# Another order of nodes over the partitions in a three-pass graph kernel: blocks of 32 nodes become runs of 8

## The reference

```python
h = relu(ln(x))
x = x + (adj.T @ h) / adj.sum(axis=0)[:, None]     # layer 0
h = relu(ln(x))
x1 = silu((adj @ h) @ W + b)                       # layer 1, first multiplication
x2 = silu((adj @ x1) @ W + b)                      # layer 1, second multiplication
return x + x2
```

## Time and profile before

| | |
|---|---|
| median of three runs | 654.42 us (653.28 to 654.83) |
| profiled execution, its own time | 653.19 us |
| its span, first to last instruction | 651.3 us |
| mean granted TensorE clock | 0.992 of full speed |
| PE, PEld, DVE, ACT, POOL busy | 627.0, 402.9, 504.0, 298.5, 562.0 us |
| moved by DMA | 199.82 MB |

### The profile page before, as it was taken

The page is one execution under the profiler, slowest core; times in us unless marked ns, Lnnn a source line. Parts: engine busy times, 40 slices in busy tenths (PEclk is TensorE's granted clock), DMA queues, the critical chain, the costliest instruction groups (busy, mean ns, idle before and its releaser), DMA issues.

```text
span 651.3 us, 6791 instructions
## 1 busy us (share of the span) xinstructions
PE 627.0 (96%) x2232; PEld 402.9 (62%) x2232; DVE 504.0 (77%) x518; ACT 298.5 (46%) x372; POOL 562.0 (86%) x283
## 2 busy tenths in 40 slices
PE   7889999999997989999999999999999999999996
PEld 5356666567574456566667667666666666665664
DVE  3988889888847889687777877777787968966982
ACT  1475433543442164645445445445444435433452
POOL 2389899499786579998999999999999999996994
PEclk8999999999998999999999999999999999999999
DMA  8999999999999999999999999909999999999971
GB/s 269 355 374 333 338 336 361 312 328 358 325 280 342 288 343 348 331 315 286 347 347 311 348 347 323 281 2 217 313 346 333 324 318 343 343 320 292 327 234 33
DMA packets 155827, 199.82 MB, mean 307 GB/s; under 512 B 5520, under 2 KB 138896, under 8 KB 155792
## 3 DMA queue, kind: packets, MB, share of 16 engines
q1 hardware_dynamic: 91568, 136.07, 66.4%
q10 hardware_dynamic: 64224, 63.32, 33.0%
HBM read 197.26 MB, written 2.10 MB: 306 GB/s over the span
## 4 chain that ended last, share of the span: by engine, by line
PE 65%; POOL 16%; issue 8%; DMA 6%; DVE 3%; ACT 1%; SPq 1%; POOLq 0%; DVEq 0%; ACTq 0%
PE dg L391 23%; POOL a_lo L762 12%; PE dg L408 11%; PE dg L398 10%; PE dg L397 10%; PE m_ps L314 5%; DMA raw<-in_adj_dram 4%; POOL at_lo L776 3%; PE m_ps L417 2%; DMA h<-in_x_dram 2%; PE m_ps L319 1%; PE m_ps L334 1%; DVE dg L614 1%; PE m_ps L320 1%; POOL norm L743 1%
## 5 line engine op out<-in xcount | busy, mean ns | idle before, releaser
L776 POOL TENSOR_TENSOR at_lo<-turned,at_hi 128x1024 fp32r<-128x1024 f32 x160 | 379.9, 2413 | 18.7 <-ACT at_hi L509 12.3
L658 DVE STREAM_TRANSPOSE turned<-raw 128x1024 f32<-128x1024 f32 x256 | 302.4, 1222 | 79.1 <-PE dg L391 43.4
L509 ACT ACTIVATE at_hi<-turned 128x1024 fp32r<-128x1024 f32 x160 | 169.1, 1060 | 201.3 <-DVE turned L658 147.2
L391 PE MATMUL dg<-turned,f_w 128*128 128x512 f32 x384 | 180.5, 592 | 3.0 <-issue 1.8
L762 POOL TENSOR_TENSOR a_lo<-raw,a_hi 128x1024 fp32r<-128x1024 f32 x62 | 145.8, 2383 | 34.7 <-ACT a_hi L478 34.4
L614 DVE TENSOR_TENSOR dg<-raw,dg 128x2048 f32<-128x2048 f32 x60 | 137.6, 2293 | 39.4 <-DMA raw<-in_adj_dram 37.6
L397 PE MATMUL dg<-at_hi,f_hi 128*128 128x512 f32 x320 | 133.0, 416 | 0.5 <-ACT at_hi L509 0.5
L408 PE MATMUL dg<-at_lo,f_hi 128*128 128x512 f32 x320 | 130.1, 488 | 1.1 <-POOL at_lo L776 1.0
L398 PE MATMUL dg<-at_hi,f_lo 128*128 128x512 f32 x320 | 126.5, 395 | 0.0
L314 PE MATMUL m_ps<-raw,h 128*128 128x512 f32 x264 | 119.8, 601 | 6.3 <-DMA raw<-in_adj_dram 6.3
L391 PEld LDWEIGHTS dg<-turned,f_w 128*128 128x128 f32 x384 | 72.4, 189 | 58.2 <-issue 50.3
(11 more groups left out here) (50 smaller groups left out, 248.9 us busy)
## 6 DMA issues: line engine op xcount, KB each, us to landing
raw<-in_adj_dram SPq DMA_DIRECT2D x64, 1024.0 KB, 7.8
raw<-in_adj_dram SPq DMA_DIRECT2D x120, 512.0 KB, 11.8
raw<-in_adj_dram ACTq DMA_DIRECT2D x120, 512.0 KB, 12.5
x<-in_x_dram SPq DMA_DIRECT2D x16, 128.0 KB, 8.2
out_dram<-zs SPq DMA_DIRECT2D x12, 128.0 KB, 12.4
h<-in_x_dram SPq DMA_DIRECT2D x1, 768.0 KB, 9.7
h<-in_x_dram SPq DMA_DIRECT2D x1, 256.0 KB, 3.3
out_dram<-zs SPq DMA_DIRECT2D x4, 64.0 KB, 1.8
```

The source lines that it names most:

```text
L391: mm = pe.matmul(acc, f_w[:, UC * WHOLE3.index(j) + c], turned[:, unit % TURN, c], start=first and c == 0, stop=False)
L509: act.activation(at_hi[:, s % RING3], turned[:, unit % TURN], ACT.Copy).then_inc(hi3_done, 1)
L658: dve.transpose(dst, src).then_inc(t3_done, 1)
L776: pool.tensor_tensor(at_lo[:, s % RING3], turned[:, unit % TURN], at_hi[:, s % RING3].bitcast(f32), ALU.subtract).then_inc(lo3_done, 1)
```

## The change

Nodes are spread "(q p m)": partition p of quarter q holds the eight neighbouring nodes q\*1024 + p\*8 + m, m = 0 to 7, in sweep 1 and in sweep 2 alike. So one load of the features serves both, into `x` (and relu writes to `h`); the sixteen later loads are gone. The loads of the features and the stores of the output have runs of 4 KB (2 KB for half quarters). A pair of sweep 1 is now two neighbouring rows of each group of eight, 128 KB of `adj` from partition to partition where it was 16 KB. The loads of sweep 2 stay as they are, but its transposes read every eighth element of a row, 32 bytes apart, and the copies to `msgT`, `degs` and `nT` read PSUM with the same step.

```diff
-    x_tiles = x_in.rearrange("(t p) d -> p t d", p=P)
-    adj_tiles = adj.rearrange("(t p) c -> p t c", p=P)
+    adj_rows = adj.rearrange("(q p m) c -> p q m c", p=P, m=QT)
     adj_blocks = adj.rearrange("(t p) c -> p t c", p=SB)
-    nodes = "(q b m c) d -> q b c m d"
-    x_nodes = x_in.rearrange(nodes, q=QUARTERS, b=P // SB, m=QT, c=SB)
-    out_nodes = out.rearrange(nodes, q=QUARTERS, b=P // SB, m=QT, c=SB)
+    x_nodes = x_in.rearrange("(q p m) d -> p q m d", p=P, m=QT)
+    out_nodes = out.rearrange("(q p m) d -> p q m d", p=P, m=QT)
...
-        def store(eng, r, part, blocks):
+        def store(eng, r, part):
             q, m = ORDER[2 * r] // 2, tiles(r, part)
             eng.wait_ge(y_ready, r - QUARTERS + part + 1)
-            for b in blocks:
-                eng.dma_start(out_nodes[q, b][:, m], zs[b * SB:(b + 1) * SB, r % 2, m]).then_inc(y_out[r % 2], 16)
+            eng.dma_start(out_nodes[:, q, m], zs[:, r % 2, m]).then_inc(y_out[r % 2], 16)
 
         def turned_nodes(dst, half=None):
-            blocks = slice(0, P // SB) if half is None else slice(2 * half, 2 * half + 2)
-            return dst.rearrange("p (m b c) -> p b m c", b=P // SB, c=SB)[:, blocks]
+            nodes = slice(0, P) if half is None else slice(half * P // 2, (half + 1) * P // 2)
+            return dst.rearrange("d (m p) -> d m p", p=P)[:, :, nodes]
 
         def natural(src):
-            return src.rearrange("p (b m c) -> p b m c", m=QT, c=SB)
+            return src.rearrange("d (p m) -> d m p", m=QT)
...
-                sp.dma_start(raw1[:, v % RAW1], adj_tiles[:, 2 * k:2 * k + 2, q * QC:(q + 1) * QC])\
+                rows, m = 2 * k // QT, 2 * k % QT
+                sp.dma_start(raw1[:, v % RAW1], adj_rows[:, rows, m:m + 2, q * QC:(q + 1) * QC])\
                   .then_inc(raw1_loaded[v % RAW1], 16)
 
-            for b, (lo, hi) in enumerate(HEAD):
-                sp.dma_start(h[:, lo:hi], x_tiles[:, lo:hi]).then_inc(x_loaded[b], 16)
-                load1(b)
-            for v in range(len(HEAD), QUARTERS * PAIRS):
+            def load_nodes(b, q, m0, m1):
+                sp.dma_start(x[:, q * QT + m0:q * QT + m1], x_nodes[:, q, m0:m1]).then_inc(x_loaded[b], 16)
+
+            load_nodes(0, 0, 0, QT // 2)
+            load1(0)
+            load_nodes(1, 0, QT // 2, QT)
+            load_nodes(1, 1, 0, QT)
+            load1(1)
+            load1(2)
+            load_nodes(2, 2, 0, QT)
+            load_nodes(2, 3, 0, QT)
+            for v in range(3, QUARTERS * PAIRS):
                 load1(v)
                 if v in PIECE0_SP:
                     load3(sp, 0, SP_BLOCKS[PIECE0_SP.index(v):][:1])
-                if v % PAIRS in NODES_AT:
-                    q, b = v // PAIRS, NODES_AT.index(v % PAIRS)
-                    sp.dma_start(x[b * SB:(b + 1) * SB, q * QT:(q + 1) * QT], x_nodes[q, b])\
-                      .then_inc(nodes_loaded[q], 16)
...
                 for t in (2 * k, 2 * k + 1):
                     if k in splits1:
-                        relu(h_hi[:, 2 * SPLIT_ROWS.index(k) + t % 2], h[:, t], t)
-                    relu(h[:, t], h[:, t], t).then_inc(h_ready, 1)
+                        relu(h_hi[:, 2 * SPLIT_ROWS.index(k) + t % 2], x[:, t], t)
+                    relu(h[:, t], x[:, t], t).then_inc(h_ready, 1)
...
-                src = raw3[i % RAW3][:, :, m * SB:(m + UC) * SB].rearrange("p t (m c) -> p m t c", c=SB)
+                src = raw3[i % RAW3].rearrange("p t (c m) -> p m t c", m=QT)[:, m:m + UC]
                 dst = turned[:, unit % TURN].rearrange("p m (t r) -> p m t r", r=SB)
                 dve.transpose(dst, src).then_inc(t3_done, 1)
```

More of the change, by code:

```diff
@@ L23 @@
 SPLIT_ROWS = (6, 8, 9, 11, 12, 14) + LATE_ROWS
-NODES_AT = (3, 6, 9, 12)
 SB = 32
@@ L120, in build @@
         x_loaded = [sem(f"x_loaded{b}") for b in range(len(HEAD))]
-        nodes_loaded = [sem(f"nodes_loaded{q}") for q in range(QUARTERS)]
         w_loaded, b_loaded = sem("w_loaded"), sem("b_loaded")
@@ L286, in _ @@
                 if i in STORE_AT:
-                    store(sp, GROUPS // 2 + STORE_AT.index(i), 0, range(P // SB))
-            for part in parts(GROUPS - 1):
-                store(sp, GROUPS - 1, part, SP_BLOCKS)
+                    store(sp, GROUPS // 2 + STORE_AT.index(i), 0)
+            store(sp, GROUPS - 1, 0)
             for r in (0, 1):
-                sp.wait_ge(y_out[r], 16 * (P // SB) * sum(len(parts(n)) for n in range(QUARTERS + r, GROUPS, 2)))
+                sp.wait_ge(y_out[r], 16 * sum(len(parts(n)) for n in range(QUARTERS + r, GROUPS, 2)))
         @block.tensor
@@ L577, in _ @@
                 silu(GROUPS - 1, part)
-            for part in parts(GROUPS - 1):
-                store(act, GROUPS - 1, part, ACT_BLOCKS)
+            store(act, GROUPS - 1, 1)
         @block.vector
@@ L601, in head @@
             def head(b):
-                dve.wait_ge(x_loaded[b], 16)
-                statistics(h, range(*HEAD[b]), b).then_inc(mv_ready, 1)
+                dve.wait_ge(x_loaded[b], 16 if b == 0 else 32)
+                statistics(x, range(*HEAD[b]), b).then_inc(mv_ready, 1)
             def add_degrees(v):
@@ L634, in add_message @@
                 dve.wait_ge(inv_ready, q + 1)
-                if part == 0:
-                    dve.wait_ge(nodes_loaded[q], 16 * (P // SB))
                 for m in range(QT // 2):
@@ L667, in add_bias @@
                 elif r >= QUARTERS + 2:
-                    dve.wait_ge(y_out[r % 2], 16 * (P // SB))
+                    dve.wait_ge(y_out[r % 2], 16)
                 dve.tensor_tensor(zs[:, r % 2, m], m_ps[:, :].rearrange("p (t d) -> p t d", d=P)[:, m],
```

## The result

The changed kernel takes 768.23 us (median, 765.84 to 770.42) where the kernel before takes 654.13 in the same comparison: a ratio of 1.1744, 95% interval 1.1711 to 1.1777. The forecast was 651.5 us with a range from 646.5 to 708; the time is outside it. It lies between the two prices given for slow transposes (707 and 839).

The account below looks back on a forecast made before the run. It took matmuls to set the pace in sweep 1, TensorE and POOL to be at the limit in sweep 2. Terms -1.5 - 1.9 + 0.5 = -2.9 us gave 651.5 us, range 646.5 to 708.

Parts of the forecast that it names:

- Transposes of every eighth element: Sweep 2, 253 transposes on VectorE reading SBUF at a 32-byte step: no added time, taken as 0.
- The bounds: Price of a sweep 2 transpose with the step: from nothing (1222 ns) to twice the time per element (2264 ns).
- Against it: Objection to the slow-transpose rival: the residual's 2690 ns may come from two operands sharing a port with POOL; transposes have one.
- the doubled price: Sweep 2 transposes at 2264 ns each, VectorE the bound: 185 us more, 839 us in all; chance 0.16 for near double.
- the second one: Rival: a 32-byte step slows sweep 2's transposes and VectorE becomes the bound; 707 or 839 us, chance 0.29.
- Its two cases: The slow-transpose rival's split in sweep 2: near double, chance 0.16, or between 1.55 and 1.75 us a transpose, chance 0.13.
- The start: Start of sweep 1: pair 2 loaded ahead of the last features lets TensorE start earlier, a gain of 1.5 us.
- Sixteen loads: Sixteen feature loads fewer, 2.1 MB: 0 in sweep 1's middle, a gain of 1.9 us in its last quarter.
- Stores: Output stores: nothing waits in sweep 2; the larger last store at the end loses 0.5 us.
- Pairs 128 KB apart: Rival: sweep 1's loads of `adj` pairs are read slower, at 308 GB/s; 18 us more, 672 us, chance 0.06.
- Copies out of PSUM: Copies on ACT to `nT` and on VectorE for the degrees, with the step: taken 0, at most 4 us.
- The sum's own range: Range of the summed terms for the whole kernel, without the rivals: 647 to 655 us.

Follow-up runs that it names:

- e2_step8: The kernel before with one line of the change alone, transposes of every eighth element; 776.87 us, ratio 1.1886.
- e7_short_pool: The changed kernel with POOL's subtraction in sweep 2 cut to 16 of 1024 elements; 766.38 us (one execution).
- e6_queue: The kernel before with only pair 2 moved ahead of the last features on SP's queue; 653.32 us, ratio 1.0003.
- e5_sweep1: The kernel before with the change's sweep 1 alone; the sixteen loads, transposes and stores stay as before; 651.98 us, ratio 0.9967.
- before: The kernel without the change; 654.13 us in the comparison with the changed kernel.
- e3_step4: The kernel before with transposes that read every fourth element, 16 bytes apart; 752.73 us (one execution).
- e4_step2: The kernel before with transposes that read every second element, 8 bytes apart; 651.62 us (one execution).
- e8_stores: The kernel before with the change's stores alone, one DMA of 512 KB in 4 KB runs for four of 128 KB; 650.46 us, ratio 0.9943.
- e1_contig: The changed kernel with one line undone, its transposes reading 32 neighbouring elements again; 643.38 us against 653.92, ratio 0.984.
- after: The changed kernel, whole change applied to the kernel before; 768.23 us, ratio 1.1744.
- f1_step2_order: The kernel before with the change's sweep 1 and, in sweep 2, neighbour pairs per partition (8-byte transpose step, 1 KB runs); 648.24 us, again 646.15.

## Why the prediction was wrong

**The step that failed** is "Transposes of every eighth element ... I take 0". The reason given was that a transpose of neighbours handles an element at the rate of a plain copy out of PSUM, "the engine and not the memory's side seems to set it". That row says what bounds a read of neighbours; it says nothing of a read with a step, and it reads PSUM, where the step is free (1224 ns before and after). A statement on SBUF needed a row on SBUF, and there was none. The runs showed 2.03 us from one transpose to the next in place of 1.18, a surcharge of 0.85 us, and 123 to 125 us for the one line. The rule that the prediction itself cites from the Trainium skill ("SBUF — State Buffer", section "Door 1: The DMA port swizzle": at least two hits on a line of 16 bytes) spoke for a price, and the trace had nothing against it; that deserved more than 0.29.

**The bounds held**, and the time lay between them, but one agreement is luck. Doubling each element's time gave 2264 ns for a transpose, and the mean record is 2262; the same transposes have records of 2182 ns in `e2_step8` and 2303 in `e7_short_pool`, all at one rate of 2.03 us, 1.7 times the old one and not twice. The row of 2690 ns that seemed to support the size was a wait for POOL (see the last section), so the prediction's own "Against it" was right. The time from the doubled price, 839 us, was 71 too high. The sum counted 253 x 2.264 = 573 us of transposes; from 226 us on, VectorE was busy 514.8 us with them, 58 less, because records overlap. It counted 23 us of other work, and there were 16. The last degree sum came 7.3 us earlier in this profile. These three make 72. Where VectorE becomes the bound was placed well: before the change it was busy 320.78 of the 408 us from 232 to 640, and a surcharge of 0.85 against a slack of 0.33 leaves 0.52 x 253 = 132 us, measured 123 to 125.

**The rival that came true** is the second one, near its middle: the range had to reach it and stopped at 708, because the doubled price was left out as the 0.16 that could be spared. Its two cases, near double and 1.55 to 1.75 us, left out the 2.03 us between them. A price that is bounded by "nothing" and "double", with an engine 21% from being the bound, can hardly be cut between the two.

**The start, a gain of 1.5.** Wrong in its mechanism: pair 2 alone came 1.35 us earlier (`e6_queue`) and nothing was left of it at 45 us, where TensorE waits for POOL whatever pair 2 does. The prediction had this chain in rows 4 and priced pair 2, which isn't on it. Charging nothing for the later additions was nearly right, 0.3 us. The sweep 1 as a whole did gain 2.2 us (`e5_sweep1`), so it is the longer runs or the new rows of a pair that gain; no run told these two apart. In the traces the queue comes sooner to the last features, at 5.89 us in `e5_sweep1` and at 7.59 in `e6_queue`; they land 12.67 and 12.57 us later.

**Sixteen loads, a gain of 1.9.** Measured 2.9, with an error of about 3: right in sign, as far as can be told, but not where the prediction had it. It took 0 outside the last quarter but for two loads at the start, and some 2 us arose in the first 46 us. The last quarter's waits, from which the 1.9 and its bound of 4.7 were taken, are a poor base: with the same code in sweep 1 TensorE waited there 4.7, 3.9, 4.4, 3.2 and 1.7 us (`before`, `e2_step8`, `e3_step4`, `e4_step2`, `e8_stores`). That the middle of sweep 1 has no room agrees with TensorE's 56.00 of 56 us in both kernels.

**Stores, a loss of 0.5 at the end and "nothing waits" in sweep 2.** Wrong in sign at both places: 3.7 us gained in all, 0.6 of it at the end. The row for it was in the profile: rows 6 have 14.6 us of waits for `raw`, "only 14.6 by a load". All of them lay behind 500 us, where the stores are, and the prediction took a sum over the sweep for an even spread.

**Pairs 128 KB apart** (0.06) did not come true: sweep 1 was no slower, and `e1_contig` with such pairs is the fastest of all.

**Copies out of PSUM**, charged at 0: right, 1224 ns on VectorE, and on ACT 581 to 597 ns (`after`, `e1_contig`) for 595.

**The sum's own range** ends at 655; by the bounds given for its terms, losses of 2.6 and 1.5 us, it would be 658.5. This changes nothing here.

## What to carry to other kernels

Before a layout is changed to win longer runs for DMA, look at what each engine's read becomes in bytes from element to element: for fp32 in SBUF a step of 8 bytes was free for VectorE's transposes and one of 16 cost two thirds more, and a layout between the two ends (pairs of neighbours) kept most of the win. An engine at 80% that does one kind of instruction all the time has 0.3 us to spare for each, so a doubt about the price of that instruction is a doubt about the whole time. And ask of a small total of waits where it stands: 14.6 us behind 500 us had one cause. Ask the same of a mean: the 2690 ns were 3.15, 3.20 and 1.72 us.

## What the runs showed that was not expected

- The step costs where VectorE reads SBUF and not where it reads PSUM (1224 ns for 1024 elements with a step of 4 and of 32 bytes); ACT's copies out of PSUM took 595 ns before and 581 after. The instructions differ as well, a copy here and a transpose there, and no run separates the two.
- VectorE's addition with both operands in SBUF and POOL's subtraction take turns. The three records behind the 2690 ns last 3.15, 3.20 and 1.72 us; each was begun during a subtraction and ends 1.1 us after that one's end (the first runs from 505.31 to 508.46, the subtraction from 504.99 to 507.38), and the next subtraction then takes 3.4 us for 2.4. In `e4_step2` one that begins at 554.24, as a subtraction ends, takes 1.24 us. In the change all three begin in the last 0.3 us of a subtraction, hence 1382 ns; how much POOL works in all doesn't matter (1567 ns in `e7_short_pool`, where it is nearly idle). With one operand the transposes did not change when POOL's work was taken away.
- Stores of 512 KB in runs of 512 bytes took 8.07 us to issue in four DMAs, in runs of 1 KB 5.80, and in runs of 4 KB, in one DMA, 1.37; loads behind them on the same queue start that much later. These are the second stores of `before`, `f1_step2_order` and `e8_stores`, one execution each; the first took 6.06, 2.60 and 0.90.
- Profiles of one execution differ in sweep 1: with the same code there, the last degree sum started at 231.7, 232.7, 232.6, 229.5 and 227.6 us (`before`, `e2_step8`, `e3_step4`, `e4_step2`, `e8_stores`). The 7.3 us that sweep 1 seemed to gain in the changed kernel's profile are in part this spread; with the change's sweep 1 it started at 224.4, 225.8 and 226.9 (`after`, `e1_contig`, `e7_short_pool`), 5.1 us earlier in the mean.
